# Attention bias as a factor behind the exponential, on VectorE, in place of a matmul that adds it in PSUM

## The reference

```python
q = _normalize_kq(q)
k = _normalize_kq(k)
pos = jnp.arange(S, dtype=jnp.int32)
bucket = _rel_position_bucket(pos[None, :] - pos[:, None])
bias = rel_bias[bucket]
bias = jnp.transpose(bias, (2, 0, 1))[None]
attn = jnp.einsum('bqhd,bkhd->bhqk', q, k) + bias
attn = attn * scale[None, :, None, None]
causal = pos[None, :] - pos[:, None] < 0
attn = jnp.where(causal[None, None], attn, -1000000.0)
attn = jax.nn.softmax(attn, axis=-1)
y = jnp.einsum('bhqk,bkhd->bqhd', attn, v).reshape(B, S, E)
```

## Time and profile before

| | us |
|---|---|
| median of the 2 runs | 3026.94 (3023.8 to 3030.08) |
| the profiled execution | 3019.43 |
| span of its slowest core, core 3, from first to last instruction | 3017.9 |
| all cores | 2990.3 to 3017.9 |

### The profile page before, as it was taken

The page is one execution under the profiler, slowest core; times in us unless marked ns, Lnnn a source line. Parts: engine busy times, 40 slices in busy tenths (PEclk is TensorE's granted clock), DMA queues, the critical chain, the costliest instruction groups (busy, mean ns, idle before and its releaser), DMA issues.

```text
span 3017.9 us, 27211 instructions; the slowest of 8 cores (2990.3 to 3017.9 us)
## 1 busy us (share of the span) xinstructions
PE 2301.1 (76%) x7955; PEld 796.2 (26%) x7955; DVE 766.4 (25%) x1421; ACT 633.8 (21%) x1203; POOL 660.3 (22%) x764
## 2 busy tenths in 40 slices
PE   2458999996776677599999999976449988998422
PEld 0212444442222222122222222222113323332111
DVE  3725444344434444301111111112330000000111
ACT  1400000000012211145646556540012200210000
POOL 0011587775232111000000000003225501420000
PEclk9987999998697655558858878777659999999655
DMA  2203132233121100000100110004438613431244
GB/s 46 73 1 42 29 42 32 39 43 118 13 23 17 12 7 8 14 7 11 18 15 11 18 18 11 18 19 104 132 57 113 88 57 74 53 55 56 91 132 126
DMA packets 137139, 139.14 MB, mean 46 GB/s; under 512 B 46320, under 2 KB 116976, under 8 KB 133882
## 3 DMA queue, kind: packets, MB, share of 16 engines
q0 software_dynamic: 96320, 61.39, 15.7%
q1 hardware_dynamic: 40682, 76.00, 7.8%
HBM read 160.80 MB, written 33.69 MB: 64 GB/s over the span
## 4 chain that ended last, share of the span: by engine, by line
PE 64%; issue 10%; DVE 9%; DMA 7%; ACT 6%; POOL 2%; SPq 1%; DVEq 0%; ACTq 0%; POOLq 0%
PE pb L625 8%; PE pb L1185 8%; PE s L1020 6%; PE s L1014 6%; PE pb L973 5%; PE pb L753 4%; PE pb L856 4%; DMA asl<-accscr 3%; PE pb4b L1204 3%; ACT pt L1027 2%; PE pb7b L1204 2%; PE pb5b L625 2%; DMA accw<-accscr 2%; PE pb4b L625 2%; PE pb6b L625 2%
## 5 line engine op out<-in xcount | busy, mean ns | idle before, releaser
L1027 ACT ACTIVATE pt<-s 128x512 bf16<-128x512 f32 (+3 forms) x640 | 336.9, 533 | 349.4 <-PE s L1020 341.6
L1014 PE MATMUL s<-tst,Jmat 128*128 128x512 bf16 (+3 forms) x640 | 277.4, 433 | 36.6 <-ACT pt L1027 27.6
L1020 PE MATMUL s<-q,k 64*128 64x512 bf16 (+3 forms) x640 | 276.7, 432 | 0.0
L658 POOL TENSOR_TENSOR acc<-acc,mtmp 128x2048 f32<-128x2048 f32 x56 | 253.6, 4528 | 103.0 <-DVE mtmp L648 103.0
L1185 PE MATMUL pb<-k,ws 128*128 128x512 bf16 x1024 | 241.2, 384 | 29.9 <-DMA ws<-W 20.3
L625 PE MATMUL pb<-xn,we 128*128 128x512 bf16 x1024 | 233.4, 381 | 5.2 <-DVE cwb L598 0.3
L264 POOL DMA_DIRECT2D ws<-W x264 | 139.9, 573 | 323.6 <-PE pb L1185 260.4
L973 PE MATMUL pb<-pt,vtl 128*65 128x512 bf16 (+3 forms) x640 | 204.6, 424 | 7.5 <-ACT pt L1027 0.3
L935 DVE CAST bc<-pbc 64x512 bf16<-64x512 f32 x64 | 43.7, 683 | 642.6 <-PE pbc L930 642.6
L264 POOL DMA_DIRECT2D tst<-cscr x16 | 8.6, 539 | 681.2 <-PE s L1020 551.0
L1226 DVE TENSOR_TENSOR acw<-acw,pb4b 128x512 f32<-128x512 f32 x8 | 5.5, 687 | 558.0 <-PE pb7b L1204 379.6
(11 more groups left out here) (260 smaller groups left out, 2865.0 us busy)
## 6 DMA issues: line engine op xcount, KB each, us to landing
ws<-W POOLq DMA_DIRECT2D x264, 64.0 KB, 2.7
we<-ew POOLq DMA_DIRECT2D x128, 128.0 KB, 5.0
xt<-x SPq DMA_DIRECT2D x16, 512.0 KB, 3.8
accscr<-acc SPq DMA_DIRECT2D x8, 1024.0 KB, 3.9
tst<-cscr POOLq DMA_DIRECT2D x16, 512.0 KB, 5.5
accw<-accscr SPq DMA_DIRECT2D x8, 1024.0 KB, 7.4
accscr<-accw SPq DMA_DIRECT2D x8, 1024.0 KB, 5.0
acw<-accscr SPq DMA_DIRECT2D x16, 512.0 KB, 4.8
```

The source lines that it names most:

```text
L658: e.tensor_tensor(ACC[dout][:, :], ACC[dout][:, :], mtmp[mp][:, :], ALU.add),
L1014: e.matmul(s16[sbk][:, so:so + w], Jmat[:, :], Tst[par][:, j0:j0 + w], start=True, stop=False),
L1020: e.matmul(s16[sbk][:, 0:w], K16[c][po:po + 64, kt * 128:(kt + 1) * 128], Q16[c][po:po + 64, q:q + w], start=False, stop=True),
L1027: e.activation(Pt[pslot][:, jc:jc + w2], s16[sbk][:, 0:w2], AF.Exp),
```

## The change

The bias is no longer added to the scores ahead of the exponential; its exponential is multiplied with theirs, exp(s + b) = exp(s) exp(b).

- Setup: `cpadS` goes through one more instruction on ACT, an exponential in place over 16 x 2176 values, before it is stored.
- A new function `tflip(par)` turns the rows of `Tst[par]` round once per head: four matmuls with `Jmat` of 512 columns each, into the two `pbc` banks in turn, each followed by a copy on DVE back into `Tst[par]`. It is called once ahead of the loop for head 0, and in each head at kt = 8 for the next head.
- Each chunk loses its bias matmul (640 over the loop), so QK alone fills the bank.
- Each chunk gains a multiplication on DVE, in place, of its part of `Pt` by `Tst` (640 over the loop); PV follows on that.

```diff
@@ -368,6 +368,8 @@
     kb.op(V, lambda e: e.memset(cpadS[:, 0:128], NEG), writes=("cpadS",))
+    kb.op(S, lambda e: e.activation(cpadS[:, :], cpadS[:, :], AF.Exp),
+          reads=("cpadS",), writes=("cpadS",))
     ld(scr_d[:, :], cpadS[:, :], sem="qS", reads=("cpadS",), writes=("cscr",))
@@ -986,6 +988,20 @@
+    def tflip(par):
+        for pp in range(NP):
+            bk = pp % 2
+            kb.op(TE, lambda e, par=par, pp=pp, bk=bk:
+                  e.matmul(pbc[bk][:, 0:512], Jmat[:, :],
+                           Tst[par][:, pp * 512:(pp + 1) * 512],
+                           start=True, stop=True),
+                  reads=("Jmat", f"tst{par}"), writes=(f"pbc{bk}",))
+            kb.op(V, lambda e, par=par, pp=pp, bk=bk:
+                  e.tensor_copy(Tst[par][:, pp * 512:(pp + 1) * 512],
+                                pbc[bk][:, 0:512]),
+                  reads=(f"pbc{bk}",), writes=(f"tst{par}",))
+
+    tflip(0)
     for h in range(H):
@@ -995,6 +1011,8 @@
         for kt in range(NTT):
+            if kt == NTT // 2 and h + 1 < H:
+                tflip(1 - par)
             ktg = h * NTT + kt
@@ -1010,23 +1028,22 @@
-                kb.op(TE, lambda e, sbk=sbk, par=par, j0=jc, w=w2, so=0:
-                      e.matmul(s16[sbk][:, so:so + w], Jmat[:, :],
-                               Tst[par][:, j0:j0 + w], start=True,
-                               stop=False),
-                      reads=("Jmat", f"tst{par}"), writes=(f"s16_{sbk}",),
-                      inc=False)
                 kb.op(TE, lambda e, sbk=sbk, c=c, po=po, kt=kt, q=cs, w=w2:
                       e.matmul(s16[sbk][:, 0:w],
                                K16[c][po:po + 64, kt * 128:(kt + 1) * 128],
                                Q16[c][po:po + 64, q:q + w],
-                               start=False, stop=True),
+                               start=True, stop=True),
                 kb.op(S, lambda e, sbk=sbk, pslot=pslot, jc=jc, w2=w2:
                       e.activation(Pt[pslot][:, jc:jc + w2], s16[sbk][:, 0:w2],
                                    AF.Exp),
                       reads=(f"s16_{sbk}",), writes=(ptk,))
+                kb.op(V, lambda e, par=par, pslot=pslot, jc=jc, w2=w2:
+                      e.tensor_tensor(Pt[pslot][:, jc:jc + w2],
+                                      Pt[pslot][:, jc:jc + w2],
+                                      Tst[par][:, jc:jc + w2], ALU.mult),
+                      reads=(ptk, f"tst{par}"), writes=(ptk,))
```

## The result

| | before | after |
|---|---|---|
| median (number of runs) | 3030.08 us (11) | 3052.52 us (12) |
| ratio of after to before | | 1.0075, 95% interval 1.0046 to 1.0105 |
| profiled execution | 3019.43 us | 3052.75 us |
| span of its slowest core | 3017.9 us (core 3) | 3051.2 us (core 7) |
| first QK, length to the last QK, rest of the span | 1287.6, 736.0, 994.3 us | 1292.0, 755.1, 1004.1 us |

The kernel became slower by about 0.75%, where 3003 us and a small gain were forecast; the interval leaves out no change, on the slower side. The time itself is inside the forecast range and within 2%.

What follows compares the result with a forecast made beforehand. Attention was taken as bound by PE at half clock: 15 heads of 44.9 us plus 41.0 make 714.5 against 736.0; adding 2.2, 2.1 and 0.5 leaves -16.7 from 3019.4, so 3003 us, range 2925 to 3070.

Steps and rivals of the forecast that it cites:

- (3): Flip at kt 8: two matmuls issue, the third waits for DVE's first copy; 3.4 us in each of 15 heads.
- The flip ahead of head 0: First flip, before the attention loop: exposed, 2.2 us until PE is free.
- The sum: Attention from first to last QK 714.5 us against 736.0; with the setup and last-chunk terms, 16.7 us less in all.
- (1): PE in attention: 640 bias matmuls go, 14.5 us a head at 1.2 GHz and their loads; 36.8 us of work stays.
- (2): PE's waits for exponentials to free score banks: a head without flips takes 41.5 us at half clock.
- the slower rival: Weight loads show at each QK and PV matmul: 48.9 us a head, 3067 us in all; chance 0.13.
- (4): 640 bf16 multiplies on DVE: 0.42 us per 512 columns, 15.1 us a head, hidden behind the exponentials.
- The DVE rival: Multiplies on DVE take 692 ns each: the flip waits 0.3 us longer, 3008 us in all; chance 0.05.
- the sign named for being wrong: In attention: the forecast would be wrong, above all, if the clock stays up or PV waited for multiplies; no size given.
- (5): Setup: the exponential of cpadS on ACT lies on the path to xt's first loads and adds 2.1 us.
- The clock: PE's granted clock over attention: 0.50 to 0.60 against 0.76, since the 128-row bias matmuls are gone.
- the whole difference between no change and a clear gain: Claim that the half-clock forecast for attention alone decides this; clock at today's 0.76 would give 2929 us, chance 0.20.

Runs made afterwards that it cites:

- e2: The kernel after with both tflip calls left out, so a wrong distance's bias is multiplied in; 2965.46 us, ratio 0.9812 to before.
- e1: The kernel after with a separate buffer name for each 512-column piece of Tst; 3014.22 us, ratio 0.9972 to before.
- e11: e6 with score banks alternating across blocks and zero-padded 128-row QK already from head 2 on; 2876.00 us, ratio 0.9459 to before.
- e9: e2 with a 128-row matmul ahead of each QK, its result overwritten by QK; profiled execution 3028.54 us, no ratio.
- e5: e1 with each head's four flip pieces put one each into blocks 12 to 15 instead of all at block 8; 2966.66 us, ratio 0.9826 to before.
- e6: e5 with QK of 128 rows, 64 of Q zero, from head 4 on; 2899.33 us, ratio 0.9591 to before.

## Why the prediction was wrong

**The step that failed: (3), the flip, 3.4 us.** It measured 5.9 (after against e2), and 3.1 once the names were per piece (e1 against e2), so the working was near for a flip that waits for banks only. What it missed is that the flip matmul also reads `Tst[par]`, one name, which the copy before it writes; "PE issues two matmuls, then the third waits" was never so. This can be read in the diff: `reads=("Jmat", f"tst{par}")` in the matmul, `writes=(f"tst{par}",)` in the copy. A head came out 2.7 us longer than forecast, 2.5 of it the flip and 0.2 the rest, and 15 x 2.7 = 40.5 us turned a gain of 16.7 into a loss. The flip ahead of head 0 was mis-sized by the same thing: first matmul to first QK 5.65 us (1286.39 to 1292.04) for 2.2, and 2.66 in e1.

**The sum.** Attention 714.5 forecast, 755.1 measured, 713.9 with the names mended. That is +40.6. The other 9.3 us of the profiled execution (3052.75 against 3003) lie after the last QK: 1004.1 us to the end of the span, 994.3 before. The eight cores of after's one execution scatter from 988.9 to 1004.1 there, those of before's from 987.5 to 994.2, so it is mostly the scatter of untouched stages, and the slowest core is the one where it is longest. The cores' medians, 995.4 and 991.8, differ by 3.6 us; whether that is the change's own is left open. Ahead of the first QK the sum seems met, 4.4 us later for 4.3 forecast, but that is luck: the first flip alone took 3.4 us more than its term, and before's cores reach their first QK anywhere from 1283.3 to 1289.5. Neither touches the 40 us.

**(1) and (2), PE's steps at half clock: right.** 41.7 us a head without flip for 41.5, 40.8 for the last for 41.0. QK after QK shows no weight load: timeline of after, two 512-column QKs within 1.03 us after a PV burst, where one by itself lasts about 0.60, so the second started some 0.43 after the first.

```profile
1400.52 1.70 PE L975 MATMUL pb<-pt,vtl 128*65 128x256 bf16 x4
1402.16 1.03 PE L1032 MATMUL s<-q,k 64*128 64x512 bf16 x2
```

The rule of the Trainium skill (TensorE: Matmul & The Clock Gate, "The mechanism" under packing small matmuls), that a load overlaps only when the row group differs, would have given the slower rival, 48.9 us a head. The trace does not agree with that sentence, by the 0.43; the same section also lets a load into a background weight buffer go ahead, which would fit. After's heads at 47.6 come near the rival by their length, but for another reason: e2's 41.7 us leave no room for 10 exposed loads. To go by the sign of the result alone would have confirmed the wrong rival.

**(4) Multiply: right**, 423 ns and nearly hidden (14.3 us in all, 0.9 a head for the 0.5 counted at the flip). The DVE rival's rate of 692 ns was wrong, but DVE's bound was nearer than its price said: doubling the work cost 60 us. That PV waits for multiplies, the sign named for being wrong, did not come in after (2.5 us) and did at the higher clock of e11 (30.4).

**(5) exp(cpadS): right.** Timeline of the setup, before (core 3), then after:

```profile
42.95 0.17 DVE L370 MEMSET cpadS<- 16x128 f32 x1 [0.15 <-DVE cpadS L365]
43.19 0.33 SPq L264 DMA_DIRECT2D cscr<-cpadS  x1
```

```profile
40.47 0.17 DVE L370 MEMSET cpadS<- 16x128 f32 x1 [0.15 <-DVE cpadS L365]
40.73 2.02 ACT L371 ACTIVATE cpadS<-cpadS 16x2176 f32<-16x2176 f32 x1 [7.66 <-DVE cpadS L370]
42.82 0.33 SPq L264 DMA_DIRECT2D cscr<-cpadS  x1
```

From L370 to SP's store it is 2.35 us for 0.24: 2.1 more, as forecast. The store's own time, 42.82 for 43.19, does not show it, since L370 came 2.5 us earlier on this core.

**The clock: right.** 0.50 for the forecast 0.50 to 0.60. That the clock stayed low because of what was taken out was an expectation without a row behind it; e9 bears it out. That it is the whole difference between no change and a clear gain was too strong: e5 is 1.7% faster at 0.51. Most of the possible gain does hang on it: e6, which differs from e5 in the rows of QK (and DVE's filling of the tiles), has heads of 36.2 for 42.3 us.

## What to carry to other kernels

When a step goes PE, DVE, PE, DVE over pieces of one tile, read the names by which the program orders it before pricing the overlap: two banks bring nothing if source and target of all pieces have one name. A removed matmul may have been what kept the clock up; before taking full-array work off PE, ask what the remaining matmuls use of the array, and where half-row ones are left, try them padded with zero rows. And place helper work (here the flip) where its engine waits anyway: 0.6 us in place of 3.1, with the names mended in both.

## What the runs showed of the hardware

- Zero rows lift the clock. QK of 128 rows, half of them zeros in Q, raised the granted clock over heads 4 to 15 from 0.50 to 0.74 in after and from 0.77 to 0.92 in before, and made before 2.9% faster by itself.
- Useless work of 128 rows can pay for most of itself in clock: 14.5 us of thrown-away columns per head (at 1.2 GHz) took attention from 666.7 (e2) to 742.9 us (e9), only 4.8 us a head, because the clock went from 0.50 to 0.76 with them.
- DVE was busy 48% of attention in after (361.65 of 755.10 us), and yet a quarter of more work of the same kind came through to the time (60.5 us for some 240).
